# Label scores of a recommender: in the tail, two of five label chunks are multiplied on GpSimd and summed on ScalarE

## The reference, cut to what matters

```python
mask = jnp.sign(jnp.sum(jnp.abs(x), axis=2))[..., None]
q1 = _attn_pool(x, mask, w1, b1, w2)
q2 = _attn_pool(x, mask, w3, b3, w4)
h = jnp.concatenate([q1, q2], axis=1) @ w5 + b5
f6 = h @ w6 + b6
g = (v @ v.T)[iu, ju]                    # iu, ju: all pairs of 300 features
cross = h[:, iu] * h[:, ju] * g
f7 = cross @ w7 + b7
out8 = jnp.concatenate([f6, f7], axis=1) @ w8 + b8
return jnp.einsum('bu,bku->bk', out8, label_embedding)
```

## Time and profile before

| what | value |
|---|---|
| timed runs | 1821.87, 1830.01, 1826.41 us; median 1826.41 |
| profiled execution | 1816.68 us, its span 1814.8 us |
| busy in the span | TensorE 1581.9 us (87%), VectorE 1462.7 (81%), ScalarE 993.0 (55%), GpSimd 33.3 (2%) |
| moved by DMA | 615.16 MB, mean 339 GB/s |
| TensorE's last matmuls | about 1702 us |
| tail on VectorE | from 1684.87 us |

### The profile page before, as it was taken

How to read it: one execution, slowest core, us unless ns; L and a number is a source line. 1 busy time by engine, 2 the same in 40 slices (tenths; PEclk the granted TensorE clock), 3 DMA queues, 4 the chain that set the end, 5 groups by cost and what they waited for, 6 DMA issues and landing times.

```text
span 1814.8 us, 24816 instructions
## 1 busy us (share of the span) xinstructions
PE 1581.9 (87%) x6936; PEld 1147.5 (63%) x6936; DVE 1462.7 (81%) x5456; ACT 993.0 (55%) x2997; POOL 33.3 (2%) x62
## 2 busy tenths in 40 slices
PE   0578999999999999999999998999999999988300
PEld 0245677677777677777777776777777777755200
DVE  8978777775598899989898986667787677687996
ACT  4456676666474646565565643444444444333798
POOL 0000000000000000000000000000000000000000
PEclk9889999999999999999999999999999999999755
DMA  7397866766799999999999899989999899899895
GB/s 286 149 384 307 302 247 237 297 250 242 301 346 339 418 357 386 368 416 341 395 353 403 329 398 383 396 321 338 363 386 358 319 350 407 302 405 406 323 418 236
DMA packets 140671, 615.16 MB, mean 339 GB/s; under 512 B 17504, under 2 KB 44253, under 8 KB 110069
## 3 DMA queue, kind: packets, MB, share of 16 engines
q1 hardware_dynamic: 106181, 368.24, 53.2%
q10 hardware_dynamic: 32176, 242.32, 34.3%
q0 software_dynamic: 2176, 3.01, 0.5%
HBM read 609.70 MB, written 3.79 MB: 338 GB/s over the span
## 4 chain that ended last, share of the span: by engine, by line
PE 68%; DMA 11%; DVE 10%; ACT 9%; issue 2%; SPq 0%; ACTq 0%; POOL 0%; DVEq 0%; POOLq 0%
PE bank L615 61%; DMA wring<-in_w7p 9%; ACT stream L765 6%; DVE stream L963 3%; PE bank L568 3%; DVE junk L845 3%; DVE cring L945 2%; DMA stream<-in_x 2%; PE bank L581 1%; ACT wring L756 1%; ACT absjunk L681 1%; PE bank L626 0%; PE bank L557 0%; PE bank L595 0%; DVE wts L884 0%
## 5 line engine op out<-in xcount | busy, mean ns | idle before, releaser
L615 PE MATMUL bank<-wring,cring 128*128 128x300 f32 (+1 forms) x5616 | 1448.4, 419 | 42.0 <-ACT wring L756 29.2
L615 PEld LDWEIGHTS bank<-wring,cring 128*128 128x128 f32 (+1 forms) x5616 | 1065.2, 191 | 407.5 <-issue 41.0
L756 ACT ACTIVATE wring<-wring,gcol 128x300 f32<-128x300 f32 x1403 | 644.8, 532 | 719.1 <-DMA wring<-in_w7p 393.1
L963 DVE SCALAR_TENSOR_TENSOR stream<-stream,out 128x300 f32<-128x300 f32 x1345 | 550.7, 467 | 0.7
L945 DVE TENSOR_TENSOR cring<-lefts,sring 128x1024 f32<-128x1024 f32 (+2 forms) x312 | 372.2, 1193 | 190.4 <-PE bank L615 189.8
L845 DVE SCALAR_TENSOR_TENSOR junk<-stream,ubc 128x300 bf16<-128x300 f32 x896 | 364.5, 467 | 24.5 <-DMA stream<-in_x 24.4
L681 ACT ACTIVATE absjunk<-stream 128x300 bf16<-128x300 f32 x448 | 196.0, 440 | 3.8 <-DMA stream<-in_x 2.0
L568 PE MATMUL bank<-stream,wts 128*32 128x300 f32 x896 | 66.3, 451 | 57.6 <-DVE small L887 57.6
L963 DVE DVE_READ_ACCUMULATOR stream<-stream,out 128x1 f32 x1345 | 111.5, 83 | 0.0
L765 ACT ACTIVATE stream<-stream 128x300 f32<-128x300 f32 x255 | 111.1, 440 | 0.1
L568 PEld LDWEIGHTS bank<-stream,wts 128*32 128x32 f32 x896 | 29.8, 118 | 92.1 <-issue 67.6
(11 more groups left out here) (69 smaller groups left out, 249.5 us busy)
## 6 DMA issues: line engine op xcount, KB each, us to landing
stream<-in_label SPq DMA_DIRECT2D x320, 750.0 KB, 8.7
wring<-in_w7p ACTq DMA_DIRECT2D x169, 1200.0 KB, 8.6
stream<-in_x SPq DMA_DIRECT2D x64, 1050.0 KB, 14.5
sring<-hrows SPq DMA_DIRECT2D x152, 256.0 KB
wring<-in_w7p ACTq DMA_DIRECT2D x14, 900.0 KB, 8.3
wring<-in_w7p ACTq DMA_DIRECT2D x13, 600.0 KB, 4.1
wring<-in_w7p ACTq DMA_DIRECT2D x8, 750.0 KB, 7.9
wring<-in_w7p ACTq DMA_DIRECT2D x5, 1050.0 KB, 7.0
```

The lines of the kernel that those rows point to most:

```text
L615: mm = pe.matmul(acc[b % 4][:, 0:E], cring[0:rows, p % CSLOTS, b % 2, j0 + j, :], w, start=(p == BEGIN[b] and j == 0), stop=(p == END[b] - ...
L756: ins = nc.scalar.activation(w, w, ACT.Copy, scale=gcol[:, t:t + 1])
L963: ins = nc.vector.scalar_tensor_tensor(out=row_in, in0=row_in, scalar=1.0, in1=out8[:, m % 4, :], op0=ALU.mult, op1=ALU.mult, accum_out=sc ...
```

## The change

The table `SHARED` becomes `KIND`, a letter for each chunk: D is row form on VectorE, V a whole product on VectorE and sums on ScalarE, P a whole product on GpSimd and sums on ScalarE. From chunk 256 on the letters repeat PDPDV, and the last two chunks are D: 25 P, 27 D, 12 V, where before 51 were shared and 13 in row form. GpSimd's products have a semaphore of their own, `l_product_pool`, and ScalarE waits for the one or the other. Before its first sum of a block ScalarE now waits, as VectorE does before its first row, for the store of the block two before. The stores of blocks 6 and 7 are moved behind all products on GpSimd. VectorE reads both operands, label rows and `out8`, from SBUF as before.

```diff
-    SHARED = [n >= FIRST_SHARED and n % 5 != 4 and n < NBT * LC - 1 for n in range(NBT * LC)]
+    KIND = ["PDPDV"[(n - FIRST_SHARED) % 5] if FIRST_SHARED <= n < NBT * LC - 2 else "D" for n in range(NBT * LC)]
+
+    STORED_LAST = NBT - 2
...
     def released(n):
-        return (l_summed if SHARED[n] else l_used), sum(SHARED[k] == SHARED[n] for k in range(n + 1))
+        alone = KIND[n] == "D"
+        return (l_used if alone else l_summed), sum((KIND[k] == "D") == alone for k in range(n + 1))
+
+    def multiplied(n):
+
+        return (l_product if KIND[n] == "V" else l_product_pool), KIND[:n + 1].count(KIND[n])
...
+            def products(n):
+
+                m = n // LC
+                pool.wait_ge(out8_ready, m + 1)
+                pool.wait_ge(l_in[L_SLOT[n]], 16 * L_COUNT[n])
+                rows = lring[:, L_SLOT[n]]
+                nc.gpsimd.tensor_tensor(rows, rows, out8[:, m % 4, :].unsqueeze(1).to_broadcast([P, LR, E]),
+                                        ALU.mult).then_inc(l_product_pool, 1)
 
-            for q in range(START, STOP + 1):
+            for q in range(START, STOP):
                 for b in whole(H_OUT, q):
                     rows_out(b)
-                for m in [m for m in range(NBT) if L_END[(m + 1) * LC - 1] + 1 == q]:
+                for m in [m for m in range(STORED_LAST) if L_END[(m + 1) * LC - 1] + 1 == q]:
                     scores_out(m)
+                for n in [n for n in range(FIRST_SHARED, NBT * LC) if KIND[n] == "P" and L_END[n] == q]:
+                    products(n)
+            for m in range(STORED_LAST, NBT):
+                scores_out(m)
...
             def sums(n):
 
                 m, q0 = n // LC, n % LC * LR
-                act.wait_ge(l_product, released(n)[1])
+                act.wait_ge(*multiplied(n))
+                if m >= 2 and n == next(k for k in range(m * LC, n + 1) if KIND[k] != "D"):
+                    act.wait_ge(out_stored[m % 2], 16 * (m // 2))
...
+                if KIND[n] == "P":
+                    return
                 if r == 0:
                     dve.wait_ge(l_in[L_SLOT[n]], 16 * L_COUNT[n])
-                if SHARED[n]:
+                if KIND[n] == "V":
```

More of the change, by code:

```diff
@@ L364, in rec_kernel @@
         l_product = sem("l_product")
+        l_product_pool = sem("l_product_pool")
         l_summed = sem("l_summed")
@@ L529, in scores_out @@
             def scores_out(m):
-                ends = [max(n for n in range((m + 1) * LC) if SHARED[n] == kind) for kind in set(SHARED[:(m + 1) * LC])]
-                for n in ends:
-                    pool.wait_ge(*released(n))
+                for alone in (True, False):
+                    done = [n for n in range((m + 1) * LC) if (KIND[n] == "D") == alone]
+                    if done:
+                        pool.wait_ge(*released(done[-1]))
                 pool.dma_start(out_v[m], score[:, m % 2, :]).then_inc(out_stored[m % 2], 16)
-            for q in range(START, STOP + 1):
+            def products(n):
[6 more added lines that the diff above has]
+            for q in range(START, STOP):
                 for b in whole(H_OUT, q):
                     rows_out(b)
-                for m in [m for m in range(NBT) if L_END[(m + 1) * LC - 1] + 1 == q]:
+                for m in [m for m in range(STORED_LAST) if L_END[(m + 1) * LC - 1] + 1 == q]:
                     scores_out(m)
+                for n in [n for n in range(FIRST_SHARED, NBT * LC) if KIND[n] == "P" and L_END[n] == q]:
+                    products(n)
+            for m in range(STORED_LAST, NBT):
+                scores_out(m)
             for b in range(2):
@@ L806, in _ @@
                     out8_done(b)
-                for n in [n for n in range(FIRST_SHARED, NBT * LC) if SHARED[n] and L_END[n] == q]:
+                for n in [n for n in range(FIRST_SHARED, NBT * LC) if KIND[n] != "D" and L_END[n] == q]:
                     sums(n)
@@ L949, in label_row @@
                 n, r = m * LC + k // LR, k % LR
+                user = out8[:, m % 4, :]
                 if k == 0:
@@ L953, in label_row @@
                         dve.wait_ge(out_stored[m % 2], 16 * (m // 2))
+                if KIND[n] == "P":
+                    return
                 if r == 0:
                     dve.wait_ge(l_in[L_SLOT[n]], 16 * L_COUNT[n])
-                if SHARED[n]:
+                if KIND[n] == "V":
                     if r == 0:
                         rows = lring[:, L_SLOT[n]]
-                        nc.vector.tensor_tensor(rows, rows, out8[:, m % 4, :].unsqueeze(1).to_broadcast([P, LR, E]),
+                        nc.vector.tensor_tensor(rows, rows, user.unsqueeze(1).to_broadcast([P, LR, E]),
                                                 ALU.mult).then_inc(l_product, 1)
@@ L963, in label_row @@
                 ins = nc.vector.scalar_tensor_tensor(
-                    out=row_in, in0=row_in, scalar=1.0, in1=out8[:, m % 4, :], op0=ALU.mult, op1=ALU.mult,
+                    out=row_in, in0=row_in, scalar=1.0, in1=user, op0=ALU.mult, op1=ALU.mult,
                     accum_out=score[:, m % 2, k:k + 1])
```

## The result

The changed kernel takes 1840.83 us (median; 1835.64 to 1844.92), the kernel before 1820.58 us, seven runs of each: ratio 1.0107, 95% interval 1.0086 to 1.0127, some 20 us slower. The profiled execution took 1835.64 us with a span of 1833.5 us, 18.7 us over the span before.

A forecast was written before the change was run, and what follows sets the result against it. ScalarE, VectorE and loads stood within a few per cent in the tail. 1684.9 + 146.7 - 1.7 us, then 7.5 of store, gave 1837.4 (+22.6 on the span), put at 1849.0 us (+1.2%) on the median; range 1820 to 1874.

The forecast's parts named there:

- the sign: In the tail, VectorE rows stretched, or with gaps between them, of together some 60 us or more would show the prediction right.
- The likeliest case: In the tail, GpSimd products of about 3.4 us take turns fully with VectorE's instructions; 1838 to 1862 us, chance 58%.
- no collision: Rival: in the tail GpSimd runs beside VectorE without loss and the loads bound; time 1816 us, -0.6%, chance 17%.
- a part of one: Rival: GpSimd's products in the tail hold VectorE up only partly, or are cheaper; 1820 to 1833 us, chance 15%.
- the dearer product: Rival: each GpSimd product in the tail costs the 4.4 us of two selects; 1874 us, chance 10%.
- Turns for what both engines read: In the tail, VectorE's two-SBUF-operand instructions and GpSimd's SBUF-reading ones block each other fully; none to all of 85 us.
- The price of a product: One GpSimd product of 128 x 1500 elements: 3.4 us from select plus memset, between 1.3 and 4.4 us.
- The sum: Tail from 1684.9 us: GpSimd 71.4, VectorE 72.5 and 2.8 left over, 146.7 us, less 1.7 hidden at handovers.
- the 2.8 us left over from early products: Before the tail, four GpSimd products take 13.6 us; VectorE's idle time hides 10.8 us, so 2.8 remain.
- What was costed at nothing: ScalarE's waits for GpSimd's products and for an earlier store, and block 6's moved store, put at no time.
- One sign: In the tail, ScalarE idle, waiting for GpSimd, would show the prediction right; no size given.

## Why the prediction was right

**Direction and size.** Forecast were +22.6 us and 1849.0 us, from a median before of 1826.41; measured are +20.2 between medians (1820.58 and 1840.83) and +18.7 between the spans. Of the 8.2 us between 1849.0 and 1840.83, 5.8 come from the median before, which seven runs put lower than three. VectorE's instructions are stretched by 25 x 3.15 = 79 us in all, where 60 or more were named as the sign. The likeliest case occurred; no collision, a part of one, and the dearer product did not.

**Turns for what both engines read.** This was named as a choice that no row decided. (That GpSimd never computes in the trace of before while VectorE does is not quite so: its memset at 0.74 us overlaps two VectorE memsets at 0.81 and 0.85 us. These read nothing, so they decide nothing.) The runs decide it, and narrow it: VectorE waits only if it reads two operands from SBUF (operand in PSUM: none stretched) and only for a GpSimd instruction that reads SBUF (memset: none stretched; one operand read: all). That is the rule of the Trainium skill (SBUF — State Buffer, "Who interferes with whom"), and the traces agree in kind, with waits of 0 and 0 us and, for the instruction that reads, of 2.97 us; the product of the change cost 3.15. In the other direction a GpSimd product takes 3.36 us alone and up to 3.65 behind a VectorE instruction.

**The price of a product.** Taken at 3.4 us from memset and select, measured 3.36 alone. The bounds were 1.3 and 4.4; the memset of 1500 columns measured 1.35. The Trainium skill's figure (GPSIMD Engine Reference, section 3.1) gave an estimate of 3.3, and the trace agrees. The price of the select didn't carry over to the multiplication by a constant: 4.1 us against 2.2.

**The sum.** 146.7 - 1.7 us of tail were forecast, 141.9 measured. A product holds VectorE up for 3.15 us, not 3.4 - 0.08, but 22 of them lay in the tail and not 21: 69.3 us where 69.7 were put. What the measured tail lacks is the 2.8 us left over from early products. Three were through before the tail, not four, so VectorE waited 9.4 us for them; its idle time from 1640 to 1685 us went from 10.8 to 3.5 us (45 less 41.55 busy) and hid 7.3 of these. The other 2 us don't show as a later tail, which began at 1684.2 and not 1684.9. But that is in part luck: this execution was nine VectorE instructions ahead at 1640 us, before GpSimd's first product (5139 against 5130), and did nine fewer by 1685 (140 against 149), which at the rate of before is an estimated 2.7 us. So the early products were not shown to be free. The store behind it is 7.4 us (1826.1 to 1833.5), forecast 7.5.

**What was costed at nothing** cost nothing that shows: the run without products holds the moved stores, the order and ScalarE's new waits for stores, and is 0.9926 of before. Whatever fits in behind the loads, which bound that run, is not excluded. One sign was named wrongly: ScalarE waits in the changed kernel for VectorE's stretched whole products, not for GpSimd's, and GpSimd itself waits for loads (waits from 1685 us on; total, times, longest):

```profile
POOL stream L550 <- DMA stream<-in_label: 57.6, 22, 7.8
ACT stream L789 <- DVE stream L986: 50.6, 11, 5.2
```

**The other side of the sign.** The no-collision rival was put at -8 to -10 us. With the operand in PSUM it came to -0.71% (0.43 to 0.99%), 13 us, with the loads as the bound as described.

## What to carry to other kernels

Before you move elementwise work to GpSimd, look at what VectorE reads meanwhile. Beside a GpSimd instruction that reads SBUF, a VectorE instruction with both operands in SBUF waits for most of it (3.15 of 3.36 us here, 2.97 of 4.1), so a product moved off VectorE cost it 3.15 us where doing it cost 1.63; put one of VectorE's operands in PSUM, and the two run side by side. Such waits stand as busy time in the profile: compare the duration of one form before and after, and look at single instructions, since the list of waits is silent. Where three resources are within a few per cent of each other, first try to shift the mix between the two that have the work already: that gave 0.55% with one line.

## What was not expected

A GpSimd multiplication by a constant, with one operand, takes longer than one with two: mostly 4.0 to 4.3 us against 3.36 us for 128 x 1500. The start-to-start time of the two that follow each other at 1720.41 us, 3.99 us, bears it out. And it lets VectorE go about 1 us before it ends: the row that starts at 1742.74 is 2.97 us longer and so free at about 1745.7, while the GpSimd instruction runs from 1742.49 for 4.17 us, to 1746.66. The reason is not known, and ends on GpSimd are rough in the profile.
